# An adaLN block with routed experts on one core: four moves in a written order, a list that holds token numbers alone, and routing weights applied where a token's rows are combined

## What is computed

```python
h = layernorm(x) * (1 + ca) + sa                    # ca, sa, ga, cb, sb, gb: rows of silu(c) @ wmod, one per sequence
qkv = h @ w_qkv.T ; q = relu(q) ; k = relu(k) ; v padded with a row of ones
vk  = einsum("bhen,bhdn->bhed", v_pad, k)           # 16 heads of 32: one sum over all tokens of a sequence
out = einsum("bhed,bhdn->bhen", vk, q) ; out = out[:-1] / (out[-1:] + EPS)
x = x + ga * (out @ w_proj.T + b_proj)
h = layernorm(x) * (1 + cb) + sb
scores = sigmoid(h @ gate_w.T) ; idx = top_k(scores + router_bias, 2)
w = scores[idx] / sum(scores[idx])                  # two routing weights of a token
routed = sum over the token's two experts e of w_e * (silu(h @ W1[e]) * (h @ W3[e])) @ W2[e]    # 8 experts, inner size 352
shared = (silu(h @ sw1.T) * (h @ sw3.T)) @ sw2.T    # inner size 704
out = x + gb * (routed + shared)
```

## Time and profile before

| | |
|---|---|
| median of 3 runs | 1332.81 us (1329.33 to 1335.31) |
| profiled execution | 1328.03 us, span 1326.3 us |
| busy: PE, DVE, ACT, POOL | 1229.3, 664.9, 413.8, 396.9 us |
| mean granted clock of TensorE, 1 = full | 0.976 |
| last stage, 1154 to 1326.3 us: PE, DVE, POOL busy | 161.6, 83.4, 84.7 us |
| GpSimd's gathers of one y row set: first, and second with addition | 32 of 1.05 us, 32 of 1.60 us |

### The profile page before, as it was taken

One profiled execution on the slowest core, in us unless ns is written; L12 is line 12 of the kernel. 1 busy time (PEld: TensorE's weight loads), 2 busy tenths in 40 slices (PEclk: granted clock), 3 DMA queues, 4 the chain that ended last, 5 costly groups with the idle time before them and its releaser, 6 DMA issues.

```text
span 1326.3 us, 25206 instructions
## 1 busy us (share of the span) xinstructions
PE 1229.3 (93%) x9054; PEld 781.5 (59%) x9054; DVE 664.9 (50%) x1382; ACT 413.8 (31%) x869; POOL 396.9 (30%) x367
## 2 busy tenths in 40 slices
PE   6998998998997998977896999999999999989998
PEld 2645665665565665654564565656656665657675
DVE  6455877867777666577884211111111111126465
ACT  4332444433443332423333122222222222212121
POOL 2112656655654433200001011111111111056552
PEclk9998999999999999988998999999999999989999
DMA  7714687898896865733444455555565565489986
GB/s 233 210 42 128 165 192 191 197 219 167 206 214 162 235 184 166 233 124 112 139 146 129 112 130 133 142 123 141 135 129 137 128 141 130 111 224 239 253 232 173
DMA packets 269204, 219.08 MB, mean 165 GB/s; under 512 B 188496, under 2 KB 200784, under 8 KB 268572
## 3 DMA queue, kind: packets, MB, share of 16 engines
q1 hardware_dynamic: 239832, 155.31, 45.7%
q0 software_dynamic: 12848, 35.40, 12.0%
q10 hardware_dynamic: 16408, 26.77, 6.4%
HBM read 116.69 MB, written 56.94 MB: 131 GB/s over the span
## 4 chain that ended last, share of the span: by engine, by line
PE 51%; DVE 15%; POOL 10%; DMA 10%; issue 8%; ACT 3%; SPq 2%; ACTq 1%; DVEq 0%; POOLq 0%
PE ps_o L86 6%; PE ps_o L88 6%; PE ps_o L87 6%; PE ps_vs L86 5%; PE ps_vs L87 5%; PE ps_vs L88 5%; DMA xt<-g 3%; DMA wp_raw<-in_wproj_t 2%; PE ps_vh L86 2%; PE ps_vh L88 2%; PE ps_vh L87 2%; POOL ol L412 2%; DVE w_all L682 2%; POOL h L388 2%; POOL h L399 2%
## 5 line engine op out<-in xcount | busy, mean ns | idle before, releaser
L471 POOL DMA_INDIRECT g<-h_d,slot_token x71 | 67.8, 956 | 507.1 <-DMA xt<-g 350.0
L86 PE MATMUL ps_o<-w_all,xt 128*128 x568 | 178.7, 315 | 11.6 <-DMA xt<-g 11.6
L88 PE MATMUL ps_o<-w_all,xt 128*128 x568 | 178.6, 315 | 0.0
L87 PE MATMUL ps_o<-w_all,xt 128*128 x568 | 178.6, 314 | 0.0
L914 DVE TENSOR_TENSOR at<-ps_y,at 128x384 f16<-128x384 f32 x71 | 39.6, 558 | 176.5 <-ACT at L1171 176.5
L909 DVE SCALAR_TENSOR_TENSOR a<-ps_o,a 128x352 f32<-128x352 f32 x71 | 37.3, 525 | 173.1 <-PE ps_o L88 173.1
L1176 ACT ACTIVATE y<-ps_vs,slot_weight 128x512 f32<-128x512 f32 x71 | 48.8, 688 | 230.6 <-PE ps_vs L88 230.6
L86 PE MATMUL ps_qh<-ht,wqkv 128*128 128x128 f16 x512 | 88.9, 221 | 8.3 <-DVE qt L549 4.9
L88 PE MATMUL ps_qh<-ht,wqkv 128*128 128x128 f16 x512 | 88.9, 221 | 0.0
L87 PE MATMUL ps_qh<-ht,wqkv 128*128 128x128 f16 x512 | 88.9, 221 | 0.0
L86 PE MATMUL ps_kh<-s_ht,sh 128*128 128x256 f16 x256 | 71.3, 278 | 12.4 <-DMA s_ht<-h2t_d 8.9
(11 more groups left out here) (240 smaller groups left out, 3179.6 us busy)
## 6 DMA issues: line engine op xcount, KB each, us to landing
y_d<-y SPq DMA_DIRECT2D x71, 256.0 KB, 3.5
w_stage<-in_w_d ACTq DMA_DIRECT2D x64, 176.0 KB, 2.5
xb<-in_x SPq DMA_DIRECT2D x32, 256.0 KB, 3.5
xr<-in_x SPq DMA_DIRECT2D x32, 256.0 KB, 3.7
x_d<-x SPq DMA_DIRECT2D x32, 256.0 KB, 3.4
h_d<-hl SPq DMA_DIRECT2D x32, 256.0 KB, 2.6
h2t_d<-h2t SPq DMA_DIRECT2D x32, 256.0 KB, 3.4
s_xs<-x_d SPq DMA_DIRECT2D x32, 256.0 KB
```

What stands on the lines that cost most here:

```text
L86: nc.tensor.matmul(out, lh, rh, start=first, stop=False, skip_group_check=True)
L87: nc.tensor.matmul(out, lh, rl, start=False, stop=False, skip_group_check=True)
L88: return nc.tensor.matmul(out, ll, rh, start=False, stop=last, skip_group_check=True)
L471: pool.indirect_dma_start(m.g[:, t % 2, :], None, m.h2_d, bass.IndirectOffsetOnAxis(ap=m.slot_token[:, t:t + 1], axis=0)).then_inc(m.gathe ...
```

## The change

Four moves, and a new place for the routing weights:

- **Splits and mod.** Pieces 8 to 11 of the projection weights, the last, are split a step earlier, and a copy of a modulation row comes a step later.
- **s divisible by 8.** k_low and v_low, with their high halves on ACT, come right behind key_value_sums() and the centres, ahead of the statistics.
- **load_h(0) on SP**, the load of the first two transposed tiles for the shared experts (`s_ht`), stands at s = 31 behind load_sh() instead of behind the transposes.
- **Steps from s = 32 on.** DVE: multiply(q) ahead of divide(t); multiply(q+1), low(q) and add() ahead of residual() and stats2(); the w_lows at the end. PE: project_out() behind up(q+1). ACT: o_high() behind activate() and high().
- **The router** starts its placing one step earlier (add_runs at q = 25), and weigh() moves from q = 25 to q = 43. The masks start at q = 28 instead of 29; the pieces of the last expert are spread over four steps instead of three.
- **The list** holds the token number alone: `tile_is` has 71 columns instead of 213, made by one operation with two per-token scalars, and list_tokens() has two operations instead of five.
- **The weights.** ScalarE scales an expert's row by a constant. Both rows of a token are gathered plainly into two halves of a buffer, and y_sum() on DVE, called by combine() and add() for each of the 32 tiles, adds them with their weights. The second gather no longer waits for the first.

The diff's core:

```diff
-SPLITS_FIRST = {-2: (4,), -1: (6,), 0: (8, 9)}
-SPLITS_LAST = {-2: (5,), -1: (7,), 0: (10, 11)}
+SPLITS_FIRST = {-2: (4,), -1: (6,), 0: (10, 11)}
+SPLITS_LAST = {-2: (5,), -1: (7, 8, 9)}
-TURNS_FROM = TAIL_STEPS + 7
+TURNS_FROM = TAIL_STEPS + 6
...
         load_sh(s)
+        if s == TILES - 1:
+            sp.wait_ge(m.ht_loaded[(TILES - 1) % HT_RING], ring_use(TILES - 1, HT_RING))
+            load_h(0)
...
+            for k in range(TOP):
+                pool.indirect_dma_start(m.yb[:, r, k, :], None, m.y_d,
+                                        bass.IndirectOffsetOnAxis(ap=m.slot[:, k, order[i]:order[i] + 1], axis=0)).then_inc(m.y_loaded[i % Y_RING], 16)
-    def fetch_onto(i):
...
-                                compute_op=ALU.add).then_inc(m.y_loaded[i % Y_RING], 16)
...
+    def y_sum(t):
+        i = place_of[t]
+        r = i % YB
+        v.wait_ge(m.y_loaded[i % Y_RING], 2 * ring_use(i, Y_RING))
+        v.tensor_scalar(m.yb[:, r, 0, :], m.yb[:, r, 0, :], m.weight[:, 0, t:t + 1], None, ALU.mult).then_inc(m.y_step, 1)
+        v.wait_ge(m.y_step, 2 * i + 1)
+        v.scalar_tensor_tensor(out=m.yb[:, r, 0, :], in0=m.yb[:, r, 1, :], scalar=m.weight[:, 1, t:t + 1], in1=m.yb[:, r, 0, :],
+                               op0=ALU.mult, op1=ALU.add).then_inc(m.y_step, 1)
+        v.wait_ge(m.y_step, 2 * i + 2)
...
-            v.scalar_tensor_tensor(out=m.tile_is[:, r, k, :, :], in0=m.tile_no[:, :, :], scalar=m.tile_of[:, k, t:t + 1],
-                                   in1=m.values[:, k, t, :].unsqueeze(1).to_broadcast([P, SLOT_TILES, LISTED]),
-                                   op0=ALU.is_equal, op1=ALU.mult).then_inc(m.pair_ready, 1)
+            v.tensor_scalar(m.tile_is[:, r, k, :], m.tile_no[:, :], m.tile_of[:, k, t:t + 1], m.token_f[:, t:t + 1],
+                            ALU.is_equal, ALU.mult).then_inc(m.pair_ready, 1)
...
-        act.activation(m.y[:, t % 2, :], m.ps_ey[:, 0:C], ACT.Copy, scale=m.slot_weight[:, t:t + 1]).then_inc(m.ey_ready, 1)
+        act.activation(m.y[:, t % 2, :], m.ps_ey[:, 0:C], ACT.Copy, scale=1.0 / SCALE).then_inc(m.ey_ready, 1)
```

More of the change, by code:

```diff
@@ L738, in vector_program @@
             split_low(n)
-        if s == -1:
+        if s <= 0 or s % BT:
+            v_low(s)
+        if s == 0:
             v.wait_ge(m.mod_done, 2)
             v.tensor_scalar(m.mod[:, C:2 * C], m.ps_o[0:B, 0, :], 1.0, None, ALU.add).then_inc(m.mod_copied, 1)
-        v_low(s)
         if s < TILES:
             divide(t)
+        if s >= TILES:
+            multiply(q + 1)
+            low(q)
+            if add_due(q + 1):
+                add((q + 1) // SH_TILES - 1)
         residual(t - 1)
@@ L769, in vector_program @@
         if s >= TILES:
-            q = STEPS_PER_SLOT * (s - TILES)
-            for p in w_turn(q):
-                w_low(p)
-            multiply(q + 1)
-            low(q)
-            if add_due(q + 1):
-                add((q + 1) // SH_TILES - 1)
-            for p in w_turn(q + 1):
+            for p in (*w_turn(q), *w_turn(q + 1)):
                 w_low(p)
@@ L1089, in scalar_program @@
         q_high(s - 1)
+        if s > 0 and s % BT == 0:
+            k_high(s)
         scale(s + 2)
         scale2(t - 2)
+        if s > 0 and s % BT == 0:
+            v_high(s)
         if s == -2:
@@ L1105, in scalar_program @@
             split_high(n)
+            if s == -1 and n < 9:
+                load_stage(n + 3)
         if s == -2:
@@ L1368, in tensor_program @@
                 down((q + 1) // SH_TILES - 1)
+            project_out(t - 1)
         logits(t - 3)
```

89 lines of the change are left out of this document (37 added, 52 removed).

## The result

The changed kernel takes **1376.17 us** (median of 4 runs, 1370.14 to 1378.71) against 1334.06 (4 runs) of the kernel before: **1.0311** [1.0281, 1.0342]. It is slower by 42 us, where no change was forecast. The profiled execution of after is the one of 1370.14 us.

What follows compares the result with a forecast made beforehand. It took PE's idle stretches outside full queues, with the half clock behind them, as what bounds the kernel. 1328 - 32 of gains + 30 for the last stage = 1326, plus 4.8 to the median: 1331 us, range 1313 to 1349.

Steps and rivals of the forecast that it cites:

- Splits: Query projection: splitting its weights a step earlier takes 2 us off PE's 3.3 us wait, between 0 and 3.3.
- Every eighth tile: Key and value halves ahead of the statistics: 6 us of the sums' 8.8 us waits plus 1.5 of clock, 7.5.
- The first shared load: Load moved up SP's queue: 8.9 us wait and 2 of clock go, new 3.1 wait and 1.7 clock; net 6.
- Steps from tile 32: New order there: 3.2 us off the transposed outputs' waits and 2.3 off chunk ends, sum 5.5; bounds 1 and 9.
- Router and list: Router a step earlier, masks of 71 columns at 0.2 us: gain 11 us before the experts; bounds 5 and 16.
- a list no cheaper: Rival: 71-column masks cost what 213 do, the router gives 5 instead of 11, 1337 us; chance 0.06.
- The sums: Last stage: DVE's sums at 1.225 us a tile stall PE; 29.4 us, plus 1.2 at the end and 5 of clock.
- that rival is out: Rival of a dear multiply: it takes 0.69 us, 1.47 a tile in the last stage, 1343 us; chance 0.17.
- the low row: Profile row of 0.407 us for a single-input 512-column operation from SBUF, basis for the sum's multiply at 0.41.
- The wait taken away: Chunk 9: the first combine's 6.9 us wait for the accumulating gather goes; 2 us plus 3.4 of clock, -5.5.
- a multiply that waits for GpSimd: Rival: last-stage sums wait half a gather's issue, 1.73 us each, stage +47, 1348 us; chance 0.10.
- Gains whole: Rival: all gaps shrink as the order allows, gains 44, last stage only +26, 1315 us on the median's scale; chance 0.24.

Runs made afterwards that it cites:

- e5_undo_C: Changed kernel with gathers spaced (at most two tiles under way), old order at every eighth tile: 1361.25 us, against 1361.45 with the spacing alone.
- e8_B_only: Kernel before with only load_h(0) moved early, ahead of that step's other loads and the transposes: 1327.36 us, ratio 0.9959.
- e14_B_behind: Kernel before with only load_h(0) moved early, but behind that step's loads and ahead of the transposes: 1331.46 us, ratio 0.9974.
- e6_undo_E: Changed kernel with gathers spaced, old order from tile 32 on, early load kept: 1355.69 us, against 1361.45 with the spacing alone.
- e7_undo_F: Changed kernel with gathers spaced, router's steps at their old places, short list kept: 1366.82 us, against 1361.45 with the spacing alone.
- e3_moves_only: Kernel before with the four moves, without short list or new place of the weights; one piece of the router's shift left in: 1338.85 us, ratio 1.0045.

## Why the prediction was wrong, step by step

The time lies outside the range: 32 of gain came out as 6, and 30 of loss as 48. (The bounds given part by part add up to gains of 13 and 47, not 20 and 45; 6 lies below either.)

**The gains: the waits went, the time did not.** The waits for s_ht, the sums and the projection weights went or fell as forecast; those for ot fell by 1.3 instead of 3.2, the low halves' stayed, the masks' rose. What failed in most parts is the second half of the step, "what is late next", where one next wait was priced and there were more, or none was looked for. By down(3), where 21 of the gain was to be there, the six traces stand at 560.2 to 568.8 against 561.6.

- *Splits:* the wait fell to 1.5, and tile 1 began 2.8 earlier (39.7 for 42.5); a wait of 3.1 for ht, till 46.3, took it back. By tile 8 nothing was left of the 2. (Only pieces 8 and 9 moved a step ahead; 10 and 11 stayed in step 0, at an earlier place.)
- *Every eighth tile:* "what is late next is h_low of the tile after next" was the wrong next. At s = 8 it was qt; at s = 16 and 24 the logits, which wait for divide(), and that comes no earlier in the new order. e5_undo_C shows the exchange: 7.5 forecast, 0 found.
- *The first shared load:* the wait of about 3.1 for the sums' operand was right (2.7, at 428.5), its neighbour was not: 2.7 for ot at 454.9. The failed sentence is "it can go right behind the load of L166": seven entries of SP's queue were passed, wp_raw's load among them, and none was priced. e8_B_only and e14_B_behind show the chain. Alone the move is worth 2.3 at down(0) in the trace, 5.3 in the medians; 6 was forecast, bounds 3 to 9.
- *Steps from tile 32:* no trace shows the 5.5. The low halves' waits are 6.0 instead of 5.6, and the order moves the other waits only, in four of ten traces at a loss of 6 (e6_undo_E).
- *Router and list:* a mask takes 0.300 at 71 columns, by the measure that gave 0.435, against 0.2 forecast: cheaper, so the rival of a list no cheaper is out, but it saves little more than half of what was counted. But the first masks are now asked for in the same chunk in which their ranks are formed: PE waits 7.3 at 589, while DVE runs place() and name_slots(), the first mask beginning only at 595.80 behind a dozen short operations. "Come earlier by 1.1" did not count that chain. From down(3) to the experts 5.0 was gained instead of 11 in these two traces. Over all of them this is the one part that mostly held: 162.6 to 167.5 in the five with the old router and list, 154.2 to 158.0 in the eleven with the new ones, 8 at the means, and 158.3 in e7_undo_F, which has the short list alone.

**The sums: right place, mis-sized.** The stall of 3.4 a chunk behind the late multiply was forecast and stands in every chunk; y_sum measured 1.30 instead of 1.225, since the multiply took 0.48 and not 0.41 (it was nearer to the low row than to 0.69, so that rival is out). Sums, end and clock together were forecast at 29.4 + 1.2 + 5 = 35.6 and cost 39.8; 28 sums at 0.075 more make 2.1 of that; the other 2.1 is within the spread of a stage. The wait taken away was worth 6.9 for 5.5.

**The burst: not in the sum.** "GpSimd … no longer waits between them, so its queue isn't the bound" had the fact and missed its meaning. The wait of 3.50 ahead of the accumulating gather was what had spaced the gathers out. Without it 18 go in a row and the other engines stall: 14.9. The rival nearest to it, a multiply that waits for GpSimd, is refuted: 32 multiplies took 0.48 at the median, and of the 19 that ran beside a gather's issue three took 0.55 and one 0.63, the most. So 0.15 is the most that a multiply lost there. (That rival's 47 is 45 by the prediction's own terms, which changes nothing.)

**The other rivals.** *Gains whole* failed on both sides. Its own objection, that the next producer is 1 to 3 us behind, should have been the forecast: of 18.9 us of waits 17.6 stayed in e3_moves_only.

## What to carry to other kernels

Where several engines run in one written order, a wait that is removed is worth the distance to the next late producer, so follow each moved instruction through every queue it passes (SP's loads, ScalarE's conversions) before pricing it; where that was within 1 to 3 us here, nothing was gained. Ask of every wait that goes what it held back: one on GpSimd may have been what spaced its DMAs. A per-row scaling that moves off an idle engine onto the engine that frees the buffers cost nearly its whole length here, however low that engine's average share.

## What the runs showed of the hardware

Gathers issued by GpSimd one behind another every 1.25 us held up the other engines: 204 products took 42.4 us instead of 24.9, TensorE's signals reached ScalarE up to 18 us late (0.04 otherwise), and PE showed gaps of 1.0 to 1.7 us for which it waited for nothing recorded. After four gathers in a row a signal came 0.8 late, after six 2.9 and 4.0, in a row of 18 5.8 and 18. An eighth of the bytes (DMA share 0.15) left the stutter, a pause of 1.28 us behind each gather removed it, at DMA shares up to 0.99. What they share was not found.
